# Two graph layers with normalised rows on one core: x and u loaded first as one array, first tile sums three jobs ahead, the last four rows of blocks normalised together

## The reference

```
x_drop = x * (u >= 0.1) / 0.9                 # x, u: 8192 x 64
x1 = layernorm(x  + adj @ x_drop)             # adj: 8192 x 8192, f32
x2 = layernorm(x1 + adj @ (x1 @ weight) + bias)
```

## Time and profile before

| | us |
|---|---|
| median of 3 runs | 910.28 |
| lowest, highest | 909.92, 910.38 |
| the profiled execution's own time | 910.34 |
| its span | 908.6 |
| busy: PE, PE's weight loads | 877.6, 410.9 |
| busy: DVE, ACT, POOL | 540.9, 30.4, 25.1 |
| loads from HBM | 356.61 MB |

### The profile page before, as it was taken

The page is one execution under the profiler, slowest core; times in us unless marked ns, Lnnn a source line. Parts: engine busy times, 40 slices in busy tenths (PEclk is TensorE's granted clock), DMA queues, the critical chain, the costliest instruction groups (busy, mean ns, idle before and its releaser), DMA issues.

```text
span 908.6 us, 13717 instructions
## 1 busy us (share of the span) xinstructions
PE 877.6 (97%) x5754; PEld 410.9 (45%) x5754; DVE 540.9 (60%) x1043; ACT 30.4 (3%) x75; POOL 25.1 (3%) x24
## 2 busy tenths in 40 slices
PE   4799999999999999999999999999999999999996
PEld 3554233333343444535354554636446456356342
DVE  6466222116044756756676676868667768768556
ACT  0000000000000000000000000000000000000011
POOL 3000000000000000000000000000000000000123
PEclk9899999999999999999999999999999999999998
DMA  9999999999999999999999999989899999999952
GB/s 327 411 417 419 420 419 422 422 420 414 419 420 420 420 421 420 421 393 413 420 419 393 406 399 395 421 337 421 360 403 420 410 409 419 415 421 419 422 215 70
DMA packets 59085, 359.61 MB, mean 396 GB/s; under 512 B 6544, under 2 KB 14736, under 8 KB 16784
## 3 DMA queue, kind: packets, MB, share of 16 engines
q1 hardware_dynamic: 59024, 358.74, 96.3%
HBM read 356.61 MB, written 2.10 MB: 395 GB/s over the span
## 4 chain that ended last, share of the span: by engine, by line
PE 90%; DMA 4%; DVE 2%; SPq 1%; issue 1%; ACT 0%; DVEq 0%
PE psum L971 22%; PE psum L924 21%; PE psum L906 8%; PE psum L939 8%; PE psum L933 7%; PE psum L957 6%; PE psum L892 4%; PE psum L913 4%; PE psum L977 4%; DMA tiles<-adj_chunks 3%; PE psum L869 2%; DMA tiles<-adj 1%; PE psum L992 1%; PE psum L1007 1%; SPq L481 1%
## 5 line engine op out<-in xcount | busy, mean ns | idle before, releaser
L650 DVE TENSOR_TENSOR layer<-psum,layer 128x512 f32<-128x512 f32 (+1 forms) x143 | 98.6, 690 | 202.0 <-PE psum L971 102.9
L924 PE MATMUL psum<-tiles,stat 128*64 128x512 f32 x976 | 216.9, 593 | 0.8 <-DMA tiles<-adj_t 0.8
L971 PE MATMUL psum<-tiles,stat 128*64 128x512 f32 x944 | 211.7, 594 | 0.0
L924 PEld LDWEIGHTS psum<-tiles,stat 128*64 128x64 f32 x976 | 71.0, 137 | 128.2 <-issue 120.4
L971 PEld LDWEIGHTS psum<-tiles,stat 128*64 128x64 f32 x944 | 66.7, 137 | 123.5 <-issue 121.2
L941 PE MATMUL psum<-tiles,stat 128*64 128x256 f32 x360 | 92.7, 380 | 0.0
L906 PE MATMUL psum<-tiles,stat 128*64 128x256 f32 x360 | 92.4, 379 | 0.0
L908 PE MATMUL psum<-tiles,stat 128*64 128x256 f32 x360 | 92.4, 379 | 0.0
L682 DVE TENSOR_TENSOR tiles<-tiles 128x512 f32<-128x512 f32 x90 | 62.3, 692 | 40.3 <-PE psum L915 38.1
L906 PEld LDWEIGHTS psum<-tiles,stat 128*64 128x64 f32 x360 | 49.3, 137 | 40.9 <-issue 20.0
L685 DVE TENSOR_TENSOR tiles<-tiles 128x512 f32<-128x512 f32 x90 | 62.3, 692 | 3.1
(11 more groups left out here) (94 smaller groups left out, 858.6 us busy)
## 6 DMA issues: line engine op xcount, KB each, us to landing
tiles<-adj_t SPq DMA_DIRECT2D x306, 1024.0 KB, 13.0
tiles<-adj SPq DMA_DIRECT2D x12, 1024.0 KB, 18.9
tiles<-adj_chunks SPq DMA_DIRECT2D x12, 1024.0 KB, 20.9
tiles<-adj_parts SPq DMA_DIRECT2D x16, 256.0 KB, 14.5
x_res<-x SPq DMA_DIRECT2D x16, 128.0 KB, 13.4
out<-layer SPq DMA_DIRECT2D x8, 256.0 KB, 2.1
tiles<-u SPq DMA_DIRECT2D x3, 512.0 KB, 10.4
tiles<-x SPq DMA_DIRECT2D x3, 512.0 KB, 11.2
```

What stands on the lines that cost most here:

```text
L650: return dve.tensor_tensor(out=to, in0=addend, in1=to, op=ALU.add)
L924: last = pe.matmul(sum_f[i % 2][to, :], stat[:, j * C + c, 0:D], tile[:, c], start=begun.get("f") != i and c < 2, stop=ends and c >= 2, sk ...
L971: last = pe.matmul(bank[to, :], stat[:, j * C + c, D:2 * D], tile[:, c], start=c == 0, stop=c == C - 1)
```

## The change

1. x and u are laid out on the host as one array `xu` of four blocks of 1 MB, in which each partition's 8 KB are contiguous. SP issues the four ahead of every tile. Per block DVE does one `scalar_tensor_tensor` and one largest; the smallest is taken once over all of it. The multiplication by 1/0.9 goes away here and is put on the two additions of each turn, as `scalar_tensor_tensor` in place of `tensor_tensor`.
2. `part_turn` 0 stands ahead of the first job of quarter 1. The other two stay behind.
3. `early` (14, 0) is dealt out among the pieces of row 1, ahead of `first` (1, 8), and no more left to `lead`. In row 1 the order becomes: `early` (14, 0), two `first`, `chunk` and `rest` (0, 3), three `first`, `chunk` and `rest` (1, 3), three `first`; and after row 1 `chunk` and `rest` (2, 3), then `first` (2, 6) to (2, 9). At `pair` (0, 2) `lead` reaches its cap of 40 in both kernels with the same jobs left, and the rest of the list is the same.
4. The first tile sum of a `fused` job is its own function and is issued up to three tile jobs ahead of where it was, not ahead of the last `row_end` or `turn`, nor of the job that frees the slot for its tile.
5. At the end the root and 1/root of a pair follow at once on its variance. The last two pairs are added, squared and summed each, and then one variance, one root and one set of four small steps serve both; DVE multiplies and SP stores the last pair first, POOL the one before it.

```diff
+KEPT = 1.0 / (1.0 - DROP)
+AHEAD = 3
-XU_GROUPS = ((0, 1), (1, 4), (4, 8), (8, 12), (12, 16))
-XU_BEFORE = (1, 4, 5, 6)
+TURN_FIRST = (1,)
+XU = NB // PARTS
...
+            if g == 0 and q in TURN_FIRST:
+                jobs.append(("part_turn", q - 1))
             jobs.append(("part", q, g))
-            if q and g == 0:
+            if g == 0 and q and q not in TURN_FIRST:
                 jobs.append(("part_turn", q - 1))
...
-            early = [("early", r, 0) for r in range(rows_of_chunk((NB - EARLY) // PARTS - 1).stop, NB, 2)]
+            pieces += [[("early", r, 0)] for r in range(rows_of_chunk((NB - EARLY) // PARTS - 1).stop, NB, 2)]
             pieces += [late[n:n + 2] for n in range(0, len(late), 2)]
...
+        elif job[0] == "fused":
+            raw_done = done_after["raw", *job[1:]]
+            first_sums_from.append(min(raw_done, max(raw_done - AHEAD, freed_for[job[1:3], "raw"], chain_at)))
+            second_sums_from.append(raw_done)
...
-            load_xu(0)
+            for g in range(XU):
+                sp.dma_start(tiles[:, staged + g], xu[g]).then_inc(s_xu[g], 16)
...
+            for g in range(XU):
+                dve.wait_ge(s_xu[g], 16)
+                t = slice(g * PARTS * C, (g + 1) * PARTS * C)
+                dve.scalar_tensor_tensor(
+                    out=stat[:, t, 0:D].rearrange("p (b k) d -> p b k d", b=PARTS), in0=xu_stage[:, g, :, 1], scalar=DROP,
+                    in1=xu_stage[:, g, :, 0], op0=ALU.is_ge, op1=ALU.mult).then_inc(dropped, 1)
+                dve.wait_ge(dropped, g + 1)
+                dve.tensor_reduce(out=largest[:, g:g + 1], in_=stat[:, t, 0:D], axis=AX.XY,
+                                  op=ALU.max).then_inc(dve_step, 1)
+            dve.tensor_reduce(out=largest[:, XU:XU + 1], in_=stat[:, :, 0:D], axis=AX.XY, op=ALU.min).then_inc(dve_step, 1)
...
+            def first_sums(n):
+
+                slot, load = place[fused_jobs[n], fused_jobs[n][1:3]]
+                tile, right = tiles[:, slot], slice(B // 2, B)
+                dve.wait_ge(s_arrived[slot], 16 * load)
+                dve.tensor_tensor(out=tile[:, 0:2, right], in0=tile[:, 0:2, right], in1=tile[:, 2:4, right],
+                                  op=ALU.add).then_inc(first_sums_ready, 1)
...
             for job in jobs:
                 if job[0] in TILE_JOBS:
-                    while n_second_sums < len(fused_jobs) and second_sums_from[n_second_sums] <= n_tile_jobs:
-                        second_sums(n_second_sums)
-                        n_second_sums += 1
+                    while n_second_sums < len(fused_jobs):
+                        if n_second_sums < n_first_sums and second_sums_from[n_second_sums] <= n_tile_jobs:
+                            second_sums(n_second_sums)
+                            n_second_sums += 1
+                        elif n_first_sums < len(fused_jobs) and first_sums_from[n_first_sums] <= n_tile_jobs:
+                            first_sums(n_first_sums)
+                            n_first_sums += 1
+                        else:
+                            break
...
+            for k in range(2):
+                dve.wait_ge(squared, norms + k + 1)
+                dve.tensor_reduce(out=vsum[:, k], in_=output_squares(n - 1 + k), axis=AX.X, op=ALU.add).then_inc(dve_step, 1)
+            norms += 1
+            steps += 2
+            dve.wait_ge(dve_step, steps)
+            dve.tensor_scalar(var[:, :], vsum[:, :], 1.0 / D, scale[:, 1:2], ALU.mult, ALU.add).then_inc(var_ready, 1)
+            inverse_root(rstd[:, 2:4], var[:, :], root[:, :], newton[:, :], norms).then_inc(rstd_ready, 1)
+            dve.wait_ge(rstd_ready, n)
+            dve.tensor_tensor(out=output_rows(n), in0=output_rows(n), in1=over_features(rstd[:, 3]),
+                              op=ALU.mult).then_inc(last_y_ready, 1)
```

More of the change, by code:

```diff
@@ L308, in resnorm_graph_layers @@
     tile_jobs = [job for job in jobs if job[0] in TILE_JOBS]
-    second_sums_from = [done_after["raw", *job[1:]] for job in fused_jobs]
+    latest_freed, freed_for = 0, {}
+    for load in loads:
+        latest_freed = max(latest_freed, load[3])
+        freed_for[load[0], load[5]] = latest_freed
+    first_sums_from, second_sums_from, chain_at = [], [], 0
+    for job in jobs:
+        if job[0] in ("row_end", "turn"):
+            chain_at = done_after[job]
+        elif job[0] == "fused":
+            raw_done = done_after["raw", *job[1:]]
+            first_sums_from.append(min(raw_done, max(raw_done - AHEAD, freed_for[job[1:3], "raw"], chain_at)))
+            second_sums_from.append(raw_done)
     joined = []
@@ L404, in output_rows, with output_squares @@
             return layer2[:, finals[n] // 2].rearrange("p (c d) -> p c d", d=D)
-        output_squares = work[:, :].rearrange("p n c d -> p (n c) d")
+        def output_squares(n):
+            if n == len(finals) - 1:
+                return layer1[:, 0].rearrange("p (c d) -> p c d", d=D)
+            return work[:, :].rearrange("p n c d -> p (n c) d")
         s_arrived = [sem(f"tile_arrived_{n}") for n in range(SLOTS)]
         s_part = [None, *(sem(f"part_{q}_arrived") for q in range(1, PARTS))]
-        s_xu = [sem(f"xu_loaded_{n}") for n in range(len(XU_GROUPS))]
+        s_xu = [sem(f"xu_loaded_{n}") for n in range(XU)]
         s_res = [sem(f"x_res_loaded_{n}") for n in range(2)]
@@ L503, in scale_pair @@
                 pool.wait_ge(rstd_ready, n + 1)
-                pool.tensor_tensor(out=output_rows(n), in0=output_rows(n), in1=over_features(rstd[:, n % 2]),
+                pool.tensor_tensor(out=output_rows(n), in0=output_rows(n), in1=over_features(rstd[:, n % 2 if n < len(finals) - 2 else 2]),
                                    op=ALU.mult).then_inc(y_ready, 1)
@@ L592, in centre, with variance @@
                 norms += 1
-            def variance(squares, var_ap, n, eps=None):
+            def variance(squares, var_ap, n, eps=EPS):
                 dve.wait_ge(squared, norms)
[L596 to L602, removed]
@@ L610, in inverse_root @@
                                               op0=ALU.mult, op1=ALU.mult))
-                return dve.scalar_tensor_tensor(out=rstd_ap, in0=newton[:, 0:n], scalar=1.5, in1=rstd_ap,
+                return dve.scalar_tensor_tensor(out=rstd_ap, in0=newton_ap, scalar=1.5, in1=rstd_ap,
                                                 op0=ALU.add, op1=ALU.mult)
[L614 to L617, removed]
@@ L620, in _ @@
[L620 to L632, removed]
@@ L675, in second_sums @@
                     dve.wait_ge(operands_ready, 3 * n)
-                slot, load = place[fused_jobs[n], (i, j)]
-                dve.wait_ge(s_arrived[slot], 16 * load)
-                dve.tensor_tensor(out=tile[:, top, right], in0=tile[:, top, right], in1=tile[:, bottom, right],
-                                  op=ALU.add).then_inc(first_sums_ready, 1)
                 dve.wait_ge(first_sums_ready, n + 1)
@@ L853, in _ @@
                         quarters = arrived(job, job)
+                    if q == 0:
+                        pe.wait_ge(dropped, g + 1)
                     for k in range(PARTS):
```

100 lines of the change are left out of this document (49 added, 51 removed).

## The result

The changed kernel takes 902.82 us in the median (902.77 to 902.89), against 910.29 us for the kernel before on the same chip: a ratio of 0.9918, 95% interval 0.9905 to 0.9931. That is 7.5 us less; the prediction was 901.5 with a range from 899.5 to 905.3. The profiled execution took 902.77 us, and its span is 901.0 in place of 908.6.

What follows compares the result with a forecast made beforehand. The prediction saw two bounds of nearly equal height, PE's own work and the link's loads. Gains of 4.2 (start), 3.5 (sums) and 1.1 (end) make 8.8, from 910.34 to 901.5 us; range 899.5 to 905.3.

Steps and rivals of the forecast that it cites:

- Loads as the bound of the first 290 us: Up to the load landing at 290.6 us the link is never idle, so earlier loads shift all landings.
- Part 1: Start: x and u first, in long rows, bring all landings up to 290.6 us forward by 3.9 us.
- shift and hand: At the load of 290.6 us PE keeps the landings' shift plus its 0.3 us in hand: 4.2 us.
- Part 2 and 3: Transposition first and `early` (14, 0) earlier: worth nothing by themselves, though the latter removes 1.5 us of PE's load waits.
- Part 4: Five late products: first tile sums issued ahead save PE 0.7 us each, 3.5 us.
- Rival (b): Late products: sums stay late because another operation takes the moved sum's place; 905.0 us, chance 0.10.
- Rival (d): Rows 4 to 6: DVE stands at first sums for unlanded tiles, joins come late; slower; chance 0.06 with all else slower or equal.
- one of the signs that the prediction named for being wrong: DVE showing waits for loads at the line of the first sums; no size given.
- two jobs of grace: A `raw` job has the jobs `fused` and `raw` before it in which its tile lands, so DVE rarely stands.
- Part 5: Kernel's end: the last multiply begins 1.5 us sooner, the last store leaves 0.35 later than it would; gain 1.1 us.
- the lower case: Kernel's end: gain below 0.5 us if the two stores or DVE and POOL hinder each other.
- Rival (c): Start: PE's slow clock stays through quarter 1, gain there 1.0 in place of 4.2 us; 904.7 us, chance 0.05.

Runs made afterwards that it cites:

- extra1: The changed kernel with one more unused 1 MB load right behind the four x and u blocks: 905.31 us.
- extralate: The changed kernel with load 326 of 346, near the end, made twice into its own slot: 902.71 us.
- turnlast: The changed kernel with the first transposition put back behind quarter 1's first job: 902.87 us.
- oldplace: The changed kernel with `early` (14, 0) left to the planner as before: 902.88 us.
- ahead0: The changed kernel with the first tile sum issued where it was before, not ahead: 906.76 us.
- ahead6: The changed kernel with the first tile sum up to six tile jobs ahead in place of three: 907.62 us.
- oldend: The changed kernel with the end of before, every pair normalised by itself: 903.49 us.
- ahead12: The changed kernel with the first tile sum up to twelve tile jobs ahead in place of three: 966.81 us.

## Why the prediction was nearly right, step by step

**Loads as the bound of the first 290 us: right.** extra1 and extralate show it with the full 2.49 us and with nothing. The sum of what was undone is 2.2 (rows) + 3.94 (sums) + 0.67 (end) + 0.06 + 0.05 = 6.9 of 7.5 us; the missing 0.6 is about what isn't separated at the start, 0.8 by the landings. (The turns' additions with 1/0.9 weren't changed back by themselves either.)

**Part 1, "I take 3.9, nearer to 3.4": right in its cause, too large.** The shift of the landings was 3.0. One step was off. The missing 54 GB/s weren't all to be had: the window reached 405 and not 419, so that (405 - 365) x 26 / 419 = 2.5 us were won in bytes and (419 - 405) x 26 / 419 = 0.9 were not. Of these 0.9, 0.6 lie in the first 8 us, which ran at 388 even with rows of 8 KB (307 from 2 to 4 us, 393 from 4 to 6), and 0.3 in the 18 behind. The half microsecond that I added to the 3.4 came in, 2.5 + 0.5 = 3.0, but I can't say where: from 28 us on the two kernels' windows are alike within the rounding of GB/s, which over 240 us is worth 0.3 us. That it matched is luck. That PE could keep shift and hand, 3.0 + 0.3, held: 3.3.

**Part 2 and 3, worth nothing: right,** by turnlast and oldplace. But part 3 didn't take PE's waits for loads away: the 2.1 us from 85 to 135 (1.5 in the prediction, which lacks the wait of `L957`) became 1.2. The smallest over 4096 numbers took 4.41 us (4.7 expected) and ended at 19.92 (near 20).

**Part 4, 5 x 0.7 = 3.5: right.** By PE's position it is 6.77 - 3.28 = 3.49 us; by ahead0 3.94, explained above. Rival (b), sums that stay late, didn't come with three jobs and did with six. Rival (d) didn't come with three jobs: DVE stood 10.0 us in all at `L680` for three tiles, the longest 3.9, and no PE wait followed. By the letter that is one of the signs that the prediction named for being wrong, waits for loads at the first sums' line. The sign was badly chosen: such a wait costs only if PE then waits for something queued behind it. The reason that I gave against it, two jobs of grace, was a thin margin, as ahead6 shows.

**Part 5, 1.1: right to 0.3.** The chain was shortened by 5.34 - 3.64 = 1.70 us (1.5 expected). The 0.2 more is one small operation: in the kernel before and in oldend DVE's variance of 128x8 took 0.44 us while POOL multiplied, and at the end of the kernel after, where POOL stood still, 0.23 us on twice the numbers. But POOL's multiply ended 898.43 - 897.52 = 0.91 behind DVE's and not 0.35, as it ran for 1.55 and not for 1.04 us: 1.70 - 0.91 = 0.8. This had been named as the lower case ("DVE and POOL hinder each other"), though not priced.

**Rival (c), the slow clock through quarter 1, didn't come.** PE's first 32 multiplies took the slow 3.68 us, as rival (c) has it. The next 96 took 7.49 with no gap that the timeline shows, and they too began slow: by the records per microsecond, 10 in the first two microseconds of the slow 32, 9 from 18.3 to 20 us, 12 from 20 to 23 and 18 from 23 to 26. From 27.83 on each 32 took 1.97. So the slow clock lasted into the work of quarter 0, not through quarter 1. The Trainium skill (TensorE: Matmul & The Clock Gate, Part 1) has idle as the throttled state that sustained activity lifts, and the durations agree. The granted clock doesn't show it in this execution: it reads 1.00 from 2 to 28 us, where in the kernel before 3.68 us stood beside 0.50. So here the durations tell more than the clock's row, and why the row doesn't follow stays open.

In sum: 3.3 + 3.5 + 0.8 = 7.6 by the spans in place of 8.8, the 1.2 us between them being 0.9 at the start and 0.3 at the end. No size was made up for by another: both misses have the same sign.

## What to carry to other kernels

Where loads and the bound engine run at nearly the same pace, find the last place at which the engine meets a landing. In this kernel bytes moved ahead of it were worth their full time, and waits ahead of it, which the engine made good by then, nothing; bytes near the end were worth nothing either. A wait placed sooner in an in-order queue should be tested at several distances, since it holds up everything behind it, and what was free at three jobs lost its gain at six and cost 64 us at twelve. When two engines are to work at the same time on one tail, don't take their durations from records in which they worked alone.

## What the runs showed of the hardware

- POOL's multiply of 128x512 took 1.04 us alone and 1.55 beside DVE's; one of 128x256 took 1.12 beside DVE, and DVE's of 128x256 0.83 beside POOL, where one of twice the size took 0.69. DVE's variance of 128x8 took 0.44 us beside POOL's multiply and 0.23 without it.
- In rows of 8 KB from the first transfer on, the link moved 388 GB/s from 2 to 10 us, 412 to 28 us and 419 later; with rows of 1 KB for the 4 MB of x and u it moved 348 in place of 416 from 5 to 13 us, and 373 in place of 405 from 2 to 28 us.
- 32 multiplies took 3.68 us right after 13.9 us of idleness, beside a granted clock that reads 1.00.
- In ahead12 PE stood for 3.92 us up to 532.38, and the granted clock was 0.60 from 532 to 536 us; PE's busy time was 23 us longer over the span, for the same multiplies.
